# A transformer stage on one core: four W2 matmuls, O's rounding and one residual add change their places

## The reference, cut to what matters

```python
h = shift_token(x)
q, k, v = split(h @ wqkv, 3)              # 8 heads of 64
q, k = rotary_xpos(l2norm(q) * qs, l2norm(k) * ksc)
x = x + local_attention(q, k, v) @ wo     # window 128, softmax
h = layernorm(shift_token(x)) * lg + lb
a, g = split(h @ w1 + b1, 2)              # 2 x 682
x = x + (a * gelu(g)) @ w2 + b2
```

## Time and profile before

| what | value |
|---|---|
| device time, median of 3 runs | 2854.98 us (2850.06 to 2856.06) |
| device time of the profiled execution | 2850.51 us |
| its span, first to last instruction | 2848.6 us |
| PE busy | 2547.3 us (89%) |
| DVE busy | 1987.4 us (70%) |
| ACT busy | 1843.2 us (65%) |
| POOL busy | 1528.3 us (54%) |
| mean granted TensorE clock | 0.996 |

### The profile page before, as it was taken

One profiled execution on the slowest core, in us unless ns is written; L12 is line 12 of the kernel. 1 busy time (PEld: TensorE's weight loads), 2 busy tenths in 40 slices (PEclk: granted clock), 3 DMA queues, 4 the chain that ended last, 5 costly groups with the idle time before them and its releaser, 6 DMA issues.

```text
span 2848.6 us, 79930 instructions
## 1 busy us (share of the span) xinstructions
PE 2547.3 (89%) x29664; PEld 2224.7 (78%) x29664; DVE 1987.4 (70%) x6533; ACT 1843.2 (65%) x5192; POOL 1528.3 (54%) x1767
## 2 busy tenths in 40 slices
PE   7898888998888898899999888899988888999898
PEld 6787777887777787788767777788777777788778
DVE  6776677676767666677656767676766677777776
ACT  5766666666666666666454666666666666666665
POOL 5565556555555556555213555555564555555654
PEclk9999999999999999999999999999999999999999
DMA  3122011003000000004100000000003000000000
GB/s 112 31 76 72 30 34 46 24 19 109 13 2 2 2 2 24 2 2 173 46 23 25 2 2 2 2 2 2 2 2 108 32 2 17 17 17 17 17 17 24
DMA packets 75954, 82.18 MB, mean 29 GB/s; under 512 B 37552, under 2 KB 61872, under 8 KB 74416
## 3 DMA queue, kind: packets, MB, share of 16 engines
q1 hardware_dynamic: 70176, 75.51, 8.1%
q10 hardware_dynamic: 5392, 1.56, 0.2%
HBM read 49.53 MB, written 26.74 MB: 27 GB/s over the span
## 4 chain that ended last, share of the span: by engine, by line
PE 38%; DVE 19%; ACT 18%; POOL 11%; issue 9%; DMA 4%; SPq 2%; DVEq 0%; ACTq 0%; POOLq 0%
PE bank L1111 6%; PE bank L1113 5%; PE bank L1112 5%; POOL pr L631 5%; PE bank L1222 5%; ACT pT L834 5%; DVE pr L1714 5%; ACT pr L815 4%; PE bank L1147 3%; PE bank L1345 3%; DMA stt<-stt 2%; PE bank L1191 2%; POOL r L626 2%; PE bank L1510 2%; POOL r L618 2%
## 5 line engine op out<-in xcount | busy, mean ns | idle before, releaser
L631 POOL TENSOR_TENSOR pr<-pr,rden 128x384 f32<-128x384 f32 (+1 forms) x512 | 435.9, 859 | 645.3 <-DVE rden L1723 644.6
L815 ACT ACTIVATE pr<-pr,nb 128x192 f32<-128x192 f32 (+1 forms) x1024 | 439.1, 430 | 92.3 <-DVE nb L1714 92.3
L1714 DVE CUSTOM_DVE_ANT_0 pr<-bank,maskb,r 128x192 f32<-128x192 f32 (+1 forms) x1024 | 357.3, 395 | 102.5 <-POOL r L626 59.9
L1111 PE MATMUL bank<-h2T,w 128*128 128x256 f32 x1408 | 405.3, 288 | 10.1 <-DVE h2T L1749 4.8
L1112 PE MATMUL bank<-h2T,w 128*128 128x256 f32 x1408 | 394.8, 280 | 0.0
L1113 PE MATMUL bank<-h2T,w 128*128 128x256 f32 x1408 | 394.8, 280 | 0.0
L1111 PE MATMUL bank<-wqkv,hT 128*128 128x512 f32 x768 | 321.3, 418 | 60.5 <-DVE nb L1714 55.4
L663 POOL TENSOR_TENSOR uTl<-t,uTh 128x256 fp32r<-128x256 f32 x288 | 218.0, 757 | 211.4 <-ACT uTh L911 210.6
L1811 DVE SCALAR_TENSOR_TENSOR t<-bank,b,t 128x256 f32<-128x256 f32 (+1 forms) x384 | 182.8, 480 | 185.2 <-ACT t L896 103.0
L1112 PE MATMUL bank<-wqkv,hT 128*128 128x512 f32 x768 | 304.0, 396 | 0.0
L1113 PE MATMUL bank<-wqkv,hT 128*128 128x512 f32 x768 | 302.8, 394 | 0.0
(11 more groups left out here) (244 smaller groups left out, 7362.9 us busy)
## 6 DMA issues: line engine op xcount, KB each, us to landing
wqkv<-wqkv_split SPq DMA_DIRECT2D x18, 512.0 KB, 6.5
w<-w_split SPq DMA_DIRECT2D x3, 2816.0 KB, 9.6
Y<-in_x SPq DMA_DIRECT2D x8, 512.0 KB, 7.3
out<-Y SPq DMA_DIRECT2D x8, 512.0 KB, 3.6
stt<-stt SPq DMA_DIRECT2D x224, 3.0 KB
h<-out SPq DMA_DIRECT2D x7, 512.0 KB, 5.0
out<-h SPq DMA_DIRECT2D x7, 512.0 KB, 3.0
stt<-stt SPq DMA_DIRECT2D x192, 0.0 KB
```

Of the source, the lines that this page charges most:

```text
L631: e.tensor_tensor(probs(j, t), probs(j, t), rden[:, 2 * j:2 * j + 2].unsqueeze(2).to_broadcast([P, 2, w]), ALU.mult).then_inc(pn_done, 1)
L815: last = e.activation(probs(j, t)[:, g, :], probs(j, t)[:, g, :], ACT.Exp, bias=nb[:, hd:hd + 1], scale=-1.0, accum_out=den[:, hd:hd + 1])
L1111: e.matmul(out, left[0], right[0], start=first, stop=False)
L1714: m = e.tensor_tensor_reduce(probs(j, t)[:, g, :], bank[j][:, g * 256:g * 256 + w], far, r[:, t, 1, place(hd):place(hd) + 1], FAR, ALU.add ...
```

## The change

Four edits, none of which adds or removes an instruction:

- ScalarE: the evictions of bank 6 to o_sum become a function `O_first`, called at its old place (at the start of tile t for t > 1, and in tile 3 for O of tile 3). The rest of O of tile t - 1 is called behind the exponentials S0 instead of ahead of them; for t = 1 that is all of O.
- TensorE: other `cuts`. In tiles 1 to 3, W2's units 0 to 3 are issued in `fill(0)`, between the scores and QKV, instead of in `fill(1)`; tile 0 has unit 5 there, which was in `fill(1)`; and tile 3 has three units more in `fill(1)` of those that were in `fill(2)`.
- VectorE: O of tile t - 1 and, for t = 3, `LN_moments` are moved behind S3, still ahead of W2's residual add.
- VectorE: where there is a next tile, WO's residual add is moved up, between the square sums of K and Q.

```diff
 # scalar block
+            def O_first(L, b, t):
+
+                n = idx(L, b, t)
+                e.wait_ge(o_lo, at(o_lo, 2 * n))
+                e.wait_ge(pv_ps, at(pv_ps, 2 * n + 2))
+                for i in pair:
+                    cols = slice(2 * P * i, 2 * P * i + 2 * P)
+                    e.activation(o_sum[:, cols], bank[O_BANK[0]][:, cols], ACT.Copy).then_inc(o_first, 1)
+
             def O(L, b, t):
...
-                    e.wait_ge(o_lo, at(o_lo, 2 * n))
-                    e.wait_ge(pv_ps, at(pv_ps, 2 * n + 2))
-                    for i in pair:
-                        cols = slice(2 * P * i, 2 * P * i + 2 * P)
-                        e.activation(o_sum[:, cols], bank[O_BANK[0]][:, cols], ACT.Copy).then_inc(o_first, 1)
                     e.wait_ge(wo_ps, at(wo_ps, n))
...
-                    if t:
-                        O(L, b, t - 1)
+                    if t > 1:
+                        O_first(L, b, t - 1)
                     for j in range(3):
                         S(L, b, t, j)
+                        if t and j == 0:
+                            O(L, b, t - 1)
...
                     if t == 3:
+                        O_first(L, b, t)
                         O(L, b, t)
                         H2T(L, b, 0)
 # tensor block
-                    cuts = ((5, 5, 11, UNITS), (0, 0, 11, UNITS), (0, 0, 11, UNITS), (0, 0, 8, UNITS))[t]
+                    cuts = ((5, 6, 11, UNITS), (0, 4, 11, UNITS), (0, 4, 11, UNITS), (0, 4, 11, UNITS))[t]
 # vector block
                     S(L, b, t, 0)
                     if t > 1:
                         O_add(L, b, t - 1, 1)
-                    if t:
-                        O(L, b, t - 1)
                     S(L, b, t, 1)
-                    if t == 3:
-                        LN_moments(L, b, 0)
                     S(L, b, t, 2)
                     R(L, b, t, 0)
                     S(L, b, t, 3)
+                    if t:
+                        O(L, b, t - 1)
+                    if t == 3:
+                        LN_moments(L, b, 0)
                     if prev and t:
                         W2(*prev, t - 1)
...
                     if ahead and t:
                         squares(idx(*ahead), 0)
+                        WO(L, b, t - 1)
                         squares(idx(*ahead), 1)
...
                     if t:
-                        WO(L, b, t - 1)
+                        if not ahead:
+                            WO(L, b, t - 1)
                         halves(L, b, t - 1)
```

## The result

The changed kernel takes 3178.57 us in the median (3175.27 to 3182.34) against 2852.52 us of the kernel before on the same chip: ratio 1.1143, 95% interval 1.1122 to 1.1164, 326 us slower. The forecast was 3119 us, in a range of 2985 to 3180. Direction, place and mechanism are as forecast; the time is 60 us over the forecast and 1.4 us under the top of the range.

The account below looks back on a forecast made before the run. TensorE sets the period, waiting mainly for VectorE. From 2850.5 us, +144 us for W2's wait net of gains and +120 us for the clock give 3114.5 us, and 4.5 for the median: 3119 us, range 2985 to 3180.

Parts of the forecast that it names:

- The place and cause of the wait: TensorE, tiles 1 to 3: W2's first unit waits for VectorE's residual add, some 90 times, 330 to 350 us in all.
- The price of the wait: Tiles 1 to 3: net loss from W2's wait after what comes back, +144 us, bounds +120 and +183.
- the hand-made schedule: Tiles 1, 2 and 3 worked out by instruction times: 1.6, 1.5 and 2.2 us longer, 5.3 us per sequence with a predecessor.
- What comes back: PV starts 1.4 to 1.5 us earlier; six tiles without W2 gain some 2 us each, -15 us with some clock falls.
- The earlier masks: VectorE's masks 1 to 3 come 0.8 to 0.9 us earlier, so the 0.36 us stop inside QKV goes.
- The clock: QKV behind each of 90 new idle stretches runs partly at half clock: 1.33 us per tile, +120 us, bounds 0 and 153.
- the one case at 65.57: Kernel before: clock at half from 65.57 to 68.98 after 2.71 us idle, 0.54 of the 3.41 us while TensorE waited.
- The rival with two stretches per tile: The clock stays at half for two stretches per tile: another 90 x 1.5, about 3255 us, chance 0.04.
- The rival in which the clock holds: Full clock throughout despite the new idle stretches, so only the wait costs: 2999 us, chance 0.12.
- The numbers around the sum: Range 2985 to 3180 us from bounds of wait (-24, +39) and clock (-60, +33); mean clock about 0.9.
- The other side: W2's residual add comes early enough, so its units fill TensorE's idle time before QKV: about 2705 us, chance 0.05.
- The 153 us: Upper clock bound by the skill's rule: each of the 90 tiles pays one full half-clock stretch, instead of 120 us.

Follow-up runs that it names:

- the filled wait: Changed kernel with 18 extra transposes of the identity, results unused, behind the scores of tiles 1 to 3: 3009.35 us, ratio 1.0553.
- a wait of 0.7 us per tile behind the first mask: Changed kernel with W2's residual add behind the first mask, between the two O_adds: 2718.22 us, ratio 0.9542.

## Why the prediction was right, and where its size was off

- *The place and cause of the wait.* Shown. The first unit's wait for bank 7 made QKV wait for the whole mask chain of VectorE: 357.0 us in 90 places (forecast 330 to 350 us in some 90). The cuts alone bring it (3302.62 us), one unit is enough (3151.6 us), the same four units with an early read do not (2681.97 us).
- *The price of the wait.* +144 us forecast; measured 157 us with the clock held up by unused transposes, and 145 us in the one run of that kernel whose clock was about that of the kernel before (0.995). The tiles are within 0.2 us of the hand-made schedule.
- *What comes back.* PV's wait for WO's add disappears as worked out. Alone the move is worth 123 us, and the tiles without W2 show it cleanly: in the second pass's first sequence, tile 1 to tile 2 takes 13.94 us instead of 17.03. I gave 2 us for each of these six tiles and 15 us in all; the two sequences give 11.6 us, 3.4 in each tile 2, 0.5 and 3.1 in tile 1, 0.7 and 0.5 in tile 3.
- *The earlier masks.* The 0.36 us were forecast as part of the gain. They are nearly worthless, 6 us, as the probabilities then are waited for.
- *The clock.* The step that was mis-sized. "Each new idle stretch can bring a stretch of 3.41 us at half clock" was taken as 0.8 x 1.7 = 1.33 us per tile, 120 us. The mean granted clock gives 501 us at half clock, 5.6 us for each of the 90 waits, and the filled wait prices it at 169 to 181 us, 1.9 to 2.0 us per tile. That is the whole miss of 60 us. The wrong step is in the sentence "less where it begins while TensorE still waits": a fall that begins there was taken as cheaper, from the one case at 65.57, and it was dearer. Of 61 such falls 57 stayed down for 6.83 us, not 3.41. The rival with two stretches per tile had this kind of fall, with a chance of 0.04, since "there a wait for weights followed, here dense products". The trace of the kernel before speaks against that reason. It has a second fall of this length, which the earlier trace rows does not show, in a wait for weights of 4.21 us:

```profile
2155.78:2157.90 2.12, 0.00 (x0) 0.00 (x0) 1.97 (x11) 1.33 (x6) 0.00 (x0) 1.00 0.96 339
2157.94:2164.70 6.76, 4.71 (x11) 3.53 (x12) 2.29 (x16) 2.77 (x12) 1.65 (x2) 0.50 1.04 380
```

The clock fell at 2157.93, while TensorE waited; from 2159.99 on QKV's products ran with no further wait, 0.43 us apart, and the clock came back only at 2164.76. So both waits over 3.4 us that follow the program's start in that trace, 3.42 and 4.21 us, were followed by 6.83 us at half clock; of its six waits of about 2.7 us three were followed by 3.41 us and three by none. In the changed kernel long and short falls are mixed, 57 to 34, and the price lies between the forecast's 120 us and the rival's 255. What decides between the two lengths was not varied by itself. The rival in which the clock holds falls.
- *The numbers around the sum.* Two do not follow from their terms. The bounds as stated give 3119 + 39 + 33 = 3191 us at the top, not 3180, and 2999 - 24 = 2975 us at the bottom, not 2985; the result lies 1.4 us inside the stated top. That it lies inside is partly luck: the clock's term, 169 to 181 us, went over its own bound of 153, and the wait's used at most 13 of its 39 us of room. And 300 us at half clock of 3100 are a mean clock of 0.95, not "about 0.9"; that the measured 0.921 looks like a hit comes of this slip, for the 501 us behind it are two thirds more than the 300.
- *The other side.* The rival in which the units fill instead of block needed the residual add within 0.3 us of the end of the scores. Moved there by hand, it gave 2682 us; the 2705 worked out for it was close, but the change did not do that.

The rule that the forecast took from the Trainium skill, "TensorE: Matmul & The Clock Gate", section "HAM oscillation — how this bites in real kernels", was the better guide here: every group of matmuls behind a long wait starts at the low clock again. The trace agrees in the main: 89 of the 90 waits have a fall, and in 61 of them the clock was down before the first matmul. The 153 us put beside the rule in the forecast were my own price for it, one stretch of 3.41 us each; 169 to 181 us were measured, since most falls were longer.

Two things stay open: why a wait of 0.7 us per tile behind the first mask costs 36 us and not the 61.5 us listed, and whether another split of the 17 units beats four.

## What to carry to other kernels

Before work is moved forward to fill an idle stretch, look at what its first instruction waits for: a buffer is free only where the reading engine's program order has reached the read. Here a wait that had been met 4 us early at the old place became the bound at the new one, and moving the read to the head of VectorE's tile turned 326 us of loss into 170 us of gain. When a new idle stretch recurs on TensorE, price the clock as a second cost: here, with waits of 3.4 to 4.9 us, it was somewhat larger than the wait's own. And look up every fall of the clock in the trace at hand before its length is assumed; two of the five in the trace of the kernel before were of the long kind.

## What the runs showed of the hardware that was not expected

- The granted clock stayed at 0.50 for 6.83 us where the stretch began inside the wait (1002.69 to 1009.52, of which 5.49 us with matmuls), and for 3.41 us where matmuls ran all through it (965.15 to 968.56). In the changed kernel 57 of the 61 falls that began in a wait were long and none of the 28 that began behind it; with one unit it was 48 of 53 and none of 30, with the new cuts alone 34 of 59 and none of 24.
- Unused work can pay: 18 transposes per tile, 1620 in all, took the mean clock from 0.921 to 0.99 and 169 us off the time.
- Eighteen transposes of 128 columns behind each other took 2.19 us, 0.12 us each.
